# Moving one query projection up at the layers' turn, and one output projection a unit down in the last head group

## The reference, cut to what matters

```
mod = (silu(c) @ wmod)                  # six rows: sa, ca, ga, sb, cb, gb
x = x + ga0 * attention0(layernorm(x) * (1 + ca0) + sa0)
x = x + gb0 * clustered_linear(layernorm(x) * (1 + cb0) + sb0)

h = layernorm(x) * (1 + ca) + sa        # second block; the kernel calls h "hT"
q = h @ w_q                             # 32 heads of 128
k, v = h @ w_k, h @ w_v                 # 8 key/value heads of 128, 4 query heads on each
p = softmax(causal(q k^T / sqrt(128)))
x = x + ga * ((p v) @ w_o)
h2 = layernorm(x) * (1 + cb) + sb
x = x + gb * (silu(h2 @ gate^T) * (h2 @ up^T)) @ down^T     # hidden width 1792
```

## Time and profile before

| what | value |
|---|---|
| median of 3 runs | 1810.67 us (1808.18 to 1813.25) |
| the profiled execution's own time | 1810.07 us |
| its span in the trace | 1808.2 us |
| PE busy | 1778.4 us, 98% of the span |
| DVE, ACT, POOL busy | 70%, 61%, 24% |
| DMA traffic | 331.24 MB, mean 183 GB/s |
| mean granted TensorE clock | 0.996 |

### The profile page before, as it was taken

The page is one execution under the profiler, slowest core; times in us unless marked ns, Lnnn a source line. Parts: engine busy times, 40 slices in busy tenths (PEclk is TensorE's granted clock), DMA queues, the critical chain, the costliest instruction groups (busy, mean ns, idle before and its releaser), DMA issues.

```text
span 1808.2 us, 28904 instructions
## 1 busy us (share of the span) xinstructions
PE 1778.4 (98%) x8799; PEld 1483.5 (82%) x8799; DVE 1269.1 (70%) x2977; ACT 1096.2 (61%) x2648; POOL 438.3 (24%) x431
## 2 busy tenths in 40 slices
PE   6998999999999999999999999999999999999999
PEld 4666888888888888888888888888888878888887
DVE  5897787887777677766677777777777777454532
ACT  6665766666666666766667676666666664342331
POOL 2234404041323324041612123140413132011000
PEclk9899999999999999999999999999999999999999
DMA  9026667677676867687776867676777878213110
GB/s 350 7 82 233 187 186 219 203 203 217 180 226 179 224 194 201 188 264 206 223 219 194 236 184 223 200 217 195 220 218 204 235 193 271 90 45 116 40 31 24
DMA packets 239367, 331.24 MB, mean 183 GB/s; under 512 B 26008, under 2 KB 165528, under 8 KB 238880
## 3 DMA queue, kind: packets, MB, share of 16 engines
q1 hardware_dynamic: 238736, 328.93, 61.2%
q10 hardware_dynamic: 528, 1.05, 0.1%
HBM read 200.39 MB, written 129.50 MB: 182 GB/s over the span
## 4 chain that ended last, share of the span: by engine, by line
PE 95%; DVE 3%; ACT 1%; DMA 1%; issue 1%; POOL 0%; SPq 0%; DVEq 0%; ACTq 0%; POOLq 0%
PE ps L2132 28%; PE ps L2202 19%; PE ps L2185 12%; PE ps L2325 11%; PE ps L2168 10%; PE ps L2310 5%; PE ps L1257 2%; PE ps L2165 1%; PE ps L120 1%; PE ps L1165 1%; PE ps L1172 1%; DMA wm<-in_L_wmod_dram 1%; PE ps L1224 1%; PE ps L1233 0%; PE ps L2374 0%
## 5 line engine op out<-in xcount | busy, mean ns | idle before, releaser
L2132 PE MATMUL ps<-hA,wq 128*128 128x512 f32 x1536 | 378.3, 395 | 0.0
L2202 PE MATMUL ps<-wo,oT 128*128 128x512 f32 x1536 | 366.3, 389 | 0.2 <-DVE acc L2754 0.2
L2202 PEld LDWEIGHTS ps<-wo,oT 128*128 128x128 f32 x1536 | 288.1, 188 | 60.1 <-issue 0.4
L2479 ACT ACTIVATE pt<-pd 128x1280 fp32r<-128x1280 f32 x128 | 162.9, 1273 | 273.4 <-PE ps L2185 237.0
L2132 PEld LDWEIGHTS ps<-hA,wq 128*128 128x128 f32 x1536 | 279.5, 188 | 53.7
L2710 DVE CUSTOM_DVE_ANT_0 ps<-ps,mask 128x384 f32<-128x384 f32 (+7 forms) x512 | 220.6, 484 | 143.7 <-PE ps L2168 139.6
L2461 ACT ACTIVATE probs<-ps,nmax 128x384 f32<-128x384 f32 (+7 forms) x512 | 250.2, 503 | 61.6 <-DVE nmax L2710 59.1
L2469 ACT ACTIVATE probs<-probs,rinv 128x384 f32<-128x384 f32 (+7 forms) x512 | 232.6, 526 | 47.8 <-DVE rinv L2721 47.8
L2730 DVE STREAM_TRANSPOSE tp<-probs 128x384 f32<-128x384 f32 (+3 forms) x512 | 215.4, 478 | 4.4 <-ACT probs L2469 4.4
L2185 PE MATMUL ps<-pt,V 128*128 128x256 f32 (+1 forms) x896 | 216.4, 329 | 1.5 <-DVE oT L2743 0.4
L2738 DVE TENSOR_TENSOR pd<-pd,pt 128x1280 fp32r<-128x1280 f32 x128 | 193.3, 1510 | 2.6 <-ACT pt L2479 2.6
(11 more groups left out here) (268 smaller groups left out, 2739.6 us busy)
## 6 DMA issues: line engine op xcount, KB each, us to landing
turned_blocks<-tp SPq DMA_DIRECT2D x128, 640.0 KB, 3.4
pd<-turned_blocks SPq DMA_DIRECT2D x512, 160.0 KB, 3.5
wq_next<-in_L_attn_w_q_dram SPq DMA_DIRECT2D x16, 1024.0 KB, 7.1
wo_in<-in_L_attn_w_o_dram SPq DMA_DIRECT2D x15, 1024.0 KB, 9.7
turned_weights<-hf_chunk SPq DMA_DIRECT2D x168, 64.0 KB, 2.8
wm<-in_L_wmod_dram SPq DMA_DIRECT2D x4, 2048.0 KB, 15.6
turned_values<-tv SPq DMA_DIRECT2D x32, 256.0 KB, 4.0
xh_m<-turned_weights SPq DMA_DIRECT2D x28, 256.0 KB, 3.8
```

Of the source, the lines that this page charges most:

```text
L2132: last = nc.tensor.matmul(ps[:, bank, :], w[i][:, c, cols], hT[k][:, c, b * S:(b + 1) * S], start=(c == 0 and n == 0), stop=(c == DC - 1 a ...
L2202: last = nc.tensor.matmul(ps[:, bank, :], oT[x_][:, b, h, AT[r] * P:(AT[r] + 1) * P], wo[y_][:, h, :], start=(h == 0 and n == 0), stop=(h ...
L2479: nc.scalar.activation(flat(pt[:]), flat(pd[:, u % 2].bitcast(F32)), ACT.Copy).then_inc(phi_done, 1)
```

## The change

At the layers' turn TensorE makes the second head's queries, `q_project(0, 1)`, between the two halves of `turn_second`, and the first values, `v_project(0, 0)`, behind both halves; before, the two stood the other way round. ScalarE's `q_high(0, 1)` moves with it, from the end of its prologue to behind the second turned chunk. VectorE's and GpSimd's prologues keep their order.

In the last group, and only there, `out_project(14, 7)` goes from unit 4 to unit 5 on TensorE, and `add_out(14, 7)` goes from unit 4 to unit 5 on VectorE. In unit 5 it stands behind the query projection and ahead of `outputs(15, 3)`. GpSimd's and SyncE's lists are as before.

```diff
@@ TensorE, prologue
                             turn_second(pe, range(2))
+                            q_project(0, 1)
+                            turn_second(pe, range(2, DC))
                             v_project(0, 0)
-                            turn_second(pe, range(2, DC))
-                            q_project(0, 1)
                             pe.wait_ge(mods_done, MODS_LATE)
@@ TensorE, body
                                 if u == 4 and not first:
                                     out_project(g - 1, 6)
+                                if u == (5 if last else 4) and not first:
                                     out_project(g - 1, 7)
@@ ScalarE, prologue
                             modulated_2(act, 1)
+                            q_high(0, 1)
                             modulated_2(act, 2)
                             modulated_2(act, 3)
                             copy_mod(9)
-                            q_high(0, 1)
```

## The result

The changed kernel takes 1813.54 us as the median of 20 runs, the kernel before 1809.22 us in 20 runs beside them. The ratio is 1.0024, with a 95% interval of 1.0016 to 1.0032: 4.3 us slower, at least 2.9 and at most 5.8. The forecast of +3.1 us (as a median 1813.8 us) lies in that interval, at its lower end. Its profiled execution has a span of 1811.6 us and took 1813.38 us.

A forecast was written before the change was run, and what follows sets the result against it. TensorE, busy 98% of the span, was taken as the bound. The turn's -1.3 us and the last group's +4.4 us gave +3.1 us: 1813.2 us profiled, 1813.8 as a median; range for 8 in 10, 1810.0 to 1816.8.

The forecast's parts named there:

- The turn: Layers' turn: the 1.65 us wait ahead of the first scores goes; gain 1.3 us, bounds 0.8 to 1.65.
- The hidden parts: Layers' turn: last turned chunk, VectorE's values ahead of the maxima, and ScalarE's table load cause no new wait of any size.
- The wait for the weights: Last group: GpSimd's rows wait for the moved projection; TensorE waits 5.6 us, values' product of unit 4 loses 4.4 us.
- one meeting with VectorE's subtraction: Last group: one of GpSimd's four rows is lengthened beside VectorE's subtraction, price 1.11 us; loss without it 3.3, with two 5.5.
- the upper price by that rule: Last group: by the skill's shut-out rule, one meeting costs up to the subtraction's length; loss some 4.8 us.
- The second wait of 0.8 us: Last group: after out_project(15, 0), TensorE waits 0.8 us again for GpSimd's low values before outputs(15, 4).
- The clock: Rival, last group: TensorE's clock falls in the 5.6 us wait; +0.9 us, 1814.7 us; chance 0.25.
- the likeliest case: The forecast itself, without the clock's fall in the last group's wait: +3.1 us; chance 0.52.
- the price of 5 us: Clock rival's larger price, last group: clock stays low as long as in the first block, +5 us, 1818.8 us.
- That the weights are no bound: Rival, last group: the wait is filled and no other comes; up to 2.0 us won, 1807.4 us; chance 0.05.
- That part one gives nothing: Rival, layers' turn: late query projection or VectorE's values undo the gain; +4.4 us, 1815.1 us; chance 0.08.
- More meetings on GpSimd: Rival, last group: GpSimd held up in every weight row, 3.3 us more, 1817.1 us; chance 0.06.

The follow-up runs named there:

- the kernel run again: The changed kernel measured once more, nothing altered, against the kernel before: 1813.83 us against 1810.23, ratio 1.0020.
- part two alone: Only the last group's move of out_project(14, 7) and add_out(14, 7), prologues as before, against the kernel before: 1816.39 us, ratio 1.0031.
- the first trace: First profiled execution of the changed kernel with both moves: span 1811.6 us, took 1813.38 us; ratio to the kernel before, 1.0024.
- with the rows left out: Changed kernel, but GpSimd skips the last group's four weight rows and old weights are used: 1808.29 us against 1810.14 of before, ratio 0.9990.

## Why the prediction was right, point by point

**The turn.** Predicted 1.3 us, measured 1.47. The query projection began 1.15 us behind the turning instead of the values' 0.85: 0.3 us of waiting for the bank, where I had taken 0.4. The hidden parts were hidden. VectorE took the values at 170.61 to 171.33 and the maxima followed at 171.31, 0.97 us behind the first scores, as before. The first exponential came at 172.03, right behind the table load, 1.69 us behind the scores against 1.63 before.

**The wait for the weights.** This step carried the forecast, and it held in each of its terms. Where nothing else interferes it can be read off the end of the low values, counted from the scores of unit 4: in the kernel run again that is 1467.86 + 1.27 - 1440.25 = 28.9 us, so that the values' product could start at 28.9 instead of 24.4, a loss of 4.5. Predicted were 4.4. In part two alone it is 4.6, in the first trace 4.8 when the wait ahead of unit 2's product is taken off. TensorE's wait was 5.79 us, predicted 5.6. The four rows took 8.9 us (1454.82 to 1463.73), predicted 8.81, with one meeting with VectorE's subtraction in every trace with this order: 1.88 us for a cast of 0.61, or 2.52 for a low part of 1.29. By the rule that I took from the Trainium skill ("SBUF — State Buffer", Who interferes with whom), that the two shut each other out, a row's part can end only when the subtraction has: it ran from 1460.09 to 1461.97 in the first trace, and the cast begun at 1460.56 ended at 1462.44. The trace agrees within 0.2 us: by the rule the cast would have ended 0.61 us behind the subtraction, at 1462.58. A meeting cost 1.2 to 1.3 us on GpSimd, less than the whole length of the subtraction (1.5 to 1.9 us), which was the upper price by that rule.

What stands behind this product moved along, as the prediction had it: from there to the end it is 342.5, 342.2 and 342.2 us against 342.5. The second wait of 0.8 us, ahead of the product, didn't show in the changed kernel, because the slow projection covered it; with the clock up it did, 0.49 us.

**The clock.** Here the likeliest case was wrong, and so was the row that it leaned on. I gave the fall a chance of 0.25 because 16 matmuls right behind the 7.54 us wait at the start took 0.23 us each, the pace of `out_project` at the full clock. But these 16 are of another form (L1165, `128*32`). The same form took 0.12 us each at 27.55, and 0.24 at 41.90 in the changed kernel, where the granted clock was 0.50 (both lines stand behind the table of stretches). So TensorE ran at half its pace behind that wait, and the 1.00 of the clock's column there, which I took at its word, doesn't fit the matmuls. Read by its own form, the row speaks for the fall and not against it. Whether the wait had slowed TensorE or it had been slow from the start, the trace doesn't show: before the wait it had worked for 0.98 us.

In the last group the fall came in all three traces with the full wait (the first, part two alone, the kernel again), and in none where the wait was 1.9 us or filled. The price was right in kind: part of the slow projection hides behind the low values. I had set 3 us of work until the clock returns, a projection of 4.4 us and a price of 0.9; no row before the run showed the 3 us. It was low for 3.2, 4.7 and 6.0 us of work, and the projection took 4.3, 5.0 and 5.3. From the end of the low values to their product it took 0.9, 1.6 and 1.9 us, against 0.1 with the clock held, so the fall costs 0.8 to 1.8 us. That wide matmuls shorten the low stretch, as I argued against the price of 5 us, no run tests. The rule of the Trainium skill ("TensorE: Matmul & The Clock Gate", Part 1), that idling throttles the engine and work releases it, is borne out by these three waits, and by it the better forecast would have been had.

**What I didn't see.** The product of unit 2 moved up 2.72 us, and I didn't set its own inputs against its new time. In the trace of before the low probabilities ended at 1447.93 and the product was to start at 1448.45: half a microsecond of cover, on a chain that hangs on a transfer. It cost 0 to 0.9 us.

**The sum.** With -1.5 us for the turn, the three traces with the full wait come to +3.9 (the kernel again), +4.7 (part two alone, the turn taken off) and +6.1 us (the first), against 4.3 measured (2.9 to 5.8). They are made of 4.5 to 4.8 for GpSimd's chain, 0.8 to 1.8 for the clock, 0.1 from the low values to their product, and 0 or 0.9 at unit 2. The forecast of +3.1 was short by the clock. That the 1813.8 us forecast came within 0.3 us of the median is luck: the change was 1.2 us larger than forecast, and the 20 runs of before lay 1.4 us lower than the three shown.

**The rivals.** That the weights are no bound was not to be had, and its price of 2.0 us was wrong too: with the rows left out nothing is won. I had named the cause, the DMA that stays where it is, and then not put it in the price. That part one gives nothing: no. More meetings on GpSimd: at most one in every trace, never two on the rows.

## What to carry to other kernels

When an operation is moved into idle time, look for who waits for its end on the other engines, and count from there: the idle time of 2 us was real, but a 9 us job of GpSimd hung on the moved operation, and a second one, the low values, behind it. The moved operation was the last reader of a buffer that another engine had to refill; one place earlier in the same unit the move cost a quarter to a third as much. And a new wait of several microseconds on TensorE has to be priced with the slower clock behind it. To tell from a trace whether TensorE was slow, compare matmuls of one and the same form: two forms with the same time apiece hid a factor of two here.

## What the runs showed of the hardware that I had not expected

- The granted clock fell from 2.4 to 1.2 GHz in each of three traces with a wait of 5.79 us in the midst of dense work, and was still low for 3.2 to 6.0 us of matmuls. It fell 2.1, 3.6 and 4.9 us behind the last matmul. After waits of 1.86 and 1.88 us, one trace each, it stayed up; with 2.1 us so near, these two don't show that such a wait is safe.
- Behind the 7.54 us wait at the kernel's start TensorE ran at half its pace while the granted clock read 1.00: 16 matmuls of L1165 in 3.64 us, against 16 in 1.92 us at 27.55. In seven of ten traces the slow pace lasted until about 23 us, in three it ended within those 16 matmuls, and this makes the two lengths of the first block, 2.7 us apart. A single span holds this luck.
